# Two-layer graph attention on one core: two key tiles' weights of the second head group added by GpSimd, one sum visit fewer on TensorE, and a new order of the mixed phase

## The reference

```
# layer 0                                      # layer 1, per head
scores = (x Wq + bq)(x Wk + bk)^T / 16         logits = q k^T / sqrt(32) + log(clip(adj, 1e-8))
attn   = softmax(scores where adj != 0)        attn   = softmax(logits)
x1     = layernorm(x + (attn x) Wc)            out    = layernorm(x1 + (attn v) Wo + bo)
```

## Time and profile before

| | |
|---|---|
| median of three runs | 1208.09 us (1205.72 to 1211.17) |
| the profiled execution | 1208.68 us, span 1206.9 us |
| mean granted TensorE clock | 0.974 of full |
| busy share PE / DVE / POOL / ACT | 95% / 75% / 64% / 44% |
| PEld busy | 57% |
| period of one phase of the loop | 70.34 us |

### The profile page before, as it was taken

One profiled execution on the slowest core, in us unless ns is written; L12 is line 12 of the kernel. 1 busy time (PEld: TensorE's weight loads), 2 busy tenths in 40 slices (PEclk: granted clock), 3 DMA queues, 4 the chain that ended last, 5 costly groups with the idle time before them and its releaser, 6 DMA issues.

```text
span 1206.9 us, 21229 instructions
## 1 busy us (share of the span) xinstructions
PE 1142.7 (95%) x6458; PEld 684.8 (57%) x6474; DVE 905.3 (75%) x1718; ACT 526.8 (44%) x1021; POOL 766.5 (64%) x368
## 2 busy tenths in 40 slices
PE   7789999999999999999999999999999999999883
PEld 6555565655656565565646556564655656465431
DVE  4465886959688695968869596886959688795874
ACT  3234444545344454534445453444545344454431
POOL 1017487594948759494875949487594948759362
PEclk9889999999999999999999999999999999999786
DMA  3051331405133140513314051331405133140300
GB/s 131 1 138 37 106 88 43 133 18 141 50 107 85 42 133 18 142 50 107 84 43 132 18 142 50 109 83 44 131 18 144 48 109 83 44 131 18 96 27 18
DMA packets 69652, 94.67 MB, mean 78 GB/s; under 512 B 14081, under 2 KB 32769, under 8 KB 69634
## 3 DMA queue, kind: packets, MB, share of 16 engines
q1 hardware_dynamic: 69634, 94.44, 27.9%
HBM read 35.40 MB, written 8.39 MB: 36 GB/s over the span
## 4 chain that ended last, share of the span: by engine, by line
PE 41%; POOL 22%; DVE 20%; issue 12%; ACT 2%; DVEq 1%; POOLq 0%; DMA 0%; SPq 0%; ACTq 0%
POOL PR L1168 14%; DVE mx L1026 12%; PE misc L609 11%; PE scores L730 6%; PE misc L619 4%; PE values L753 3%; POOL z L1182 3%; PE misc L661 3%; PE misc L709 3%; POOL res L1151 3%; PE values L775 2%; PE denominators L753 2%; PE denominators L775 2%; DVE z L1108 2%; DVE st L1098 2%
## 5 line engine op out<-in xcount | busy, mean ns | idle before, releaser
L1168 POOL TENSOR_TENSOR PR<-PR,CLIP 128x1024 f32<-128x1024 f32 x232 | 572.6, 2494 | 339.7 <-ACT PR L868 315.7
L1026 DVE TENSOR_REDUCE mx<-misc 128x1 f32<-128x512 f32 x512 | 321.6, 680 | 92.5 <-PE misc L709 92.4
L868 ACT ACTIVATE PR<-scores 128x512 f32<-128x512 f32 x512 | 279.8, 603 | 225.3 <-PE scores L730 224.8
L730 PE MATMUL scores<-QS,KS 97*128 97x512 f32 x512 | 199.0, 463 | 7.5 <-issue 3.5
L753 PE MATMUL denominators<-PR,ones 128*32 128x512 f32 x1024 | 135.6, 601 | 6.3 <-POOL PR L1168 5.7
L730 PEld LDWEIGHTS scores<-QS,KS 97*128 97x128 f32 x512 | 89.0, 194 | 85.2 <-ACT PR L868 44.6
L753 PE MATMUL values<-PR,V 128*32 128x512 f32 x1024 | 133.2, 603 | 0.1
L709 PE MATMUL misc<-K1H,Q1H 32*128 32x512 f32 x512 | 120.9, 501 | 8.6 <-issue 3.0
L687 PE MATMUL misc<-U,P 128*128 128x257 f32 x512 | 121.8, 386 | 0.0
L1073 DVE RECIPROCAL sums_w<-sums_w 128x128 f32<-128x128 f32 x128 | 113.8, 923 | 4.2 <-ACT sums_w L881 4.2
L709 PEld LDWEIGHTS misc<-K1H,Q1H 32*128 32x128 f32 x512 | 49.2, 184 | 109.8 <-DVE mx L1026 52.7
(11 more groups left out here) (160 smaller groups left out, 1902.5 us busy)
## 6 DMA issues: line engine op xcount, KB each, us to landing
ADJ<-adj_t SPq DMA_DIRECT2D x16, 1024.0 KB, 6.1
QS<-Q1H SPq DMA_DIRECT2D x256, 64.0 KB, 2.0
KS<-K1H SPq DMA_DIRECT2D x256, 64.0 KB, 2.0
P<-x_t SPq DMA_DIRECT2D x16, 512.0 KB, 4.0
X<-x SPq DMA_DIRECT2D x16, 512.0 KB, 3.7
QS<-Q1L SPq DMA_DIRECT2D x128, 64.0 KB, 2.0
KS<-K1L SPq DMA_DIRECT2D x128, 64.0 KB, 2.0
out<-z SPq DMA_DIRECT2D x16, 512.0 KB, 2.9
```

Of the source, the lines that this page charges most:

```text
L730: pe.matmul(ST[n][:], KS[:, h, P * k:P * (k + 1)], QS[:, h, :], start=True, stop=True).then_inc(scores_filled, 1)
L868: act.activation(PR[quad % WEIGHT_BUFFERS][:, h, :], ST[n][:], ACT.Exp, scale=SCALE1).then_inc(exp_done, 1)
L1026: dve.tensor_reduce(mx1[:, g, h, t:t + 1], misc_bank(ph, "max1", g, n)[:], AX.X, ALU.max, negate=True).then_inc(misc_drained["dve"], 1)
L1168: pool.tensor_tensor(w, w, clipped, ALU.mult).then_inc(masked_pool, 1)
```

## The change

Four things change.

1. A new stage ("add", 5, pair): POOL adds the masked weights of quad 5 onto those of quad 4, in quad 4's buffer, in two instructions of 128x1024. It waits until `values1` of quad 4 has read that buffer and both quads are masked.
2. `denominators1` of quad 5 is gone; the one of quad 4, now later in the table, waits for the adds and sums both quads in one visit. PE makes 7 visits for denominators per graph in place of 8.
3. In `SCHEDULE` a second stage ("mask", 5, 1) moves one mask instruction per phase from POOL to DVE.
4. The whole `SCHEDULE` is reordered; in `LAST` only the stages around the adds change.

The rest of the code follows: waits for the masks are now made at every visit, and counts of denominators skip quad 5.

```
+ADDED = (5,)
 SCHEDULE = [
-    ("split", 0), ("split", 1), ("bias",), ("max1", 1, 0), ("q0", 0), ("reciprocal", 1, 0), ("q0", 1),
...
+    ("max1", 1, 0), ("split", 0), ("split", 1), ("max1", 1, 1), ("max1", 1, 2), ("bias",), ("q0", 0),
+    ("u", 0), ("reciprocal", 1, 0), ("q0", 1), ("scores1", 0, 0), ("u", 1), ("scores1", 0, 1),
...
 LAST = [
...
-    ("reciprocal", 0, 0), ("values1", 4), ("reciprocal", 0, 1), ("denominators1", 4), ("scores1", 6, 1),
-    ("values1", 5), ("scores1", 7, 0), ("mask", 6, 0), ("denominators1", 5), ("reciprocal", 0, 2),
-    ("scores1", 7, 1), ("values1", 6), ("reciprocal", 0, 3), ("mask", 7, 0), ("denominators1", 6),
-    ("high_output", 0), ("denominators1", 7), ("mask", 7, 1), ("values1", 7), ("normalise", 0),
-    ("sums_v", 1), ("sums_w", 1), ("low_output", 0),
+    ("add", 5, 0), ("reciprocal", 0, 0), ("values1", 4), ("reciprocal", 0, 1), ("scores1", 6, 1),
+    ("add", 5, 1), ("values1", 5), ("scores1", 7, 0), ("mask", 6, 0), ("reciprocal", 0, 2),
+    ("scores1", 7, 1), ("values1", 6), ("reciprocal", 0, 3), ("mask", 7, 0), ("denominators1", 4),
+    ("denominators1", 6), ("high_output", 0), ("denominators1", 7), ("mask", 7, 1), ("values1", 7),
+    ("normalise", 0), ("sums_v", 1), ("sums_w", 1), ("low_output", 0),
 ]
...
+            def wait_masked(ph, quad):
+                if masks(ph, False, quad) > (masks(ph, False, quad - 1) if quad else 0):
+                    pe.wait_ge(masked_pool, masks_before(ph, False) + masks(ph, False, quad))
+                if any(q == quad for q, _ in dve_masks(ph.kind)):
+                    pe.wait_ge(masked_dve, masks_before(ph, True) + masks(ph, True, quad))
...
             def values1(ph, quad):
-                sums1(ph, quad, PV, values_first(ph, quad)).then_inc(values_summed, 1)
+                wait_masked(ph, quad)
+                sums1(ph, quad, PV).then_inc(values_summed, 1)
 
             def denominators1(ph, quad):
-                sums1(ph, quad, DEN, not values_first(ph, quad)).then_inc(denominators_summed, 1)
+                if quad + 1 in ADDED:
+                    pe.wait_ge(weights_added, (ph.i * len(ADDED) + ADDED.index(quad + 1) + 1) * 2)
+                else:
+                    wait_masked(ph, quad)
+                sums1(ph, quad, DEN).then_inc(denominators_summed, 1)
...
+            def add(ph, quad, pair):
+
+                if pair == 0:
+                    pool.wait_ge(values_summed, ph.i * QUADS + quad)
+                    pool.wait_ge(masked_pool, masks_before(ph, False) + masks(ph, False, quad))
+                    if any(q in (quad - 1, quad) for q, _ in dve_masks(ph.kind)):
+                        pool.wait_ge(masked_dve, masks_before(ph, True) + masks(ph, True, quad))
+                w, total = (PR[q % WEIGHT_BUFFERS][:, 2 * pair:2 * pair + 2, :] for q in (quad, quad - 1))
+                pool.tensor_tensor(total, total, w, ALU.add).then_inc(weights_added, 1)
```

More of the change, by code:

```diff
@@ L73 @@
 SCHEDULE = [
-    ("split", 0), ("split", 1), ("bias",), ("max1", 1, 0), ("q0", 0), ("reciprocal", 1, 0), ("q0", 1),
[11 rows of a table removed]
-    ("scores1", 5, 0), ("denominators1", 3), ("sums_w", 0), ("mask", 5, 0), ("reciprocal", 0, 0),
-    ("scores1", 5, 1), ("values1", 2), ("denominators1", 4), ("values1", 3), ("sums_v", 0),
-    ("scores1", 6, 0), ("transpose", 0), ("transpose", 1), ("scores1", 6, 1), ("reciprocal", 0, 1),
[7 rows of a table removed]
+    ("max1", 1, 0), ("split", 0), ("split", 1), ("max1", 1, 1), ("max1", 1, 2), ("bias",), ("q0", 0),
+    ("u", 0), ("reciprocal", 1, 0), ("q0", 1), ("scores1", 0, 0), ("u", 1), ("scores1", 0, 1),
+    ("reciprocal", 1, 1), ("u", 2), ("reciprocal", 1, 2), ("max0", 0), ("reciprocal", 1, 3),
+    ("scores1", 1, 0), ("u", 3), ("normalise", 1), ("scores1", 1, 1), ("max0", 1), ("max0", 2),
+    ("scores1", 2, 0), ("max1", 1, 3), ("low_output", 1), ("max1", 1, 4), ("max1", 1, 5),
+    ("high_output", 1), ("max0", 3), ("skip_back",), ("scores1", 2, 1), ("project",), ("floor",),
[8 rows of a table added]
+    ("transpose", 0), ("transpose", 1), ("scores1", 6, 1), ("values1", 4), ("reciprocal", 0, 0),
+    ("reciprocal", 0, 1), ("reciprocal", 0, 2), ("mask", 5, 1), ("reciprocal", 0, 3), ("skip_front",),
[7 rows of a table added]
 ]
@@ L143 @@
 }
-BACK = ("residual", "mask", "scores1", "values1", "denominators1", "sums_v", "sums_w",
+BACK = ("residual", "mask", "add", "scores1", "values1", "denominators1", "sums_v", "sums_w",
         "reciprocal", "normalise", "high_output", "low_output", "skip_back")
@@ L421, in graph_of, with summed @@
             return ph.t if g == GROUPS - 1 else ph.i
+        def summed(quad):
+            return sum(1 for q in range(quad + 1) if q not in ADDED)
         def mask_operands(quad, pair):
@@ L731, in scores1, with sums1 @@
                               start=True, stop=True).then_inc(scores_filled, 1)
-            def sums1(ph, quad, bank, first):
+            def wait_masked(ph, quad):
[3 more added lines that the diff above has]
+                    pe.wait_ge(masked_dve, masks_before(ph, True) + masks(ph, True, quad))
+            def sums1(ph, quad, bank):
                 g, k = divmod(quad, T)
@@ L738, in sums1 @@
                     pe.wait_ge(z_added, ph.t * 2 + (1 if bank is PV else 2))
-                if first:
-                    if masks(ph, False, quad) > (masks(ph, False, quad - 1) if quad else 0):
-                        pe.wait_ge(masked_pool, masks_before(ph, False) + masks(ph, False, quad))
-                    if any(q == quad for q, _ in dve_masks(ph.kind)):
-                        pe.wait_ge(masked_dve, masks_before(ph, True) + masks(ph, True, quad))
-                    if quad == 0:
-                        pe.wait_ge(misc_drained["act"], misc.count_before(ph, "v", 1))
+                if quad == 0 and bank is PV:
+                    pe.wait_ge(misc_drained["act"], misc.count_before(ph, "v", 1))
                 if quad > 0 and k == 0:
@@ L1184, in output @@
                 pool.tensor_tensor(z[:], z[:], all_rows(S_B1), ALU.add).then_inc(out_ready, 1)
-            do = {"prepare": prepare, "residual": residual, "scores1": mask, "stats0": rstd0_of,
+            do = {"prepare": prepare, "residual": residual, "scores1": mask, "add": add, "stats0": rstd0_of,
                   "stats1": rstd1_of, "output": output}
```

8 lines of the change are left out of this document (3 added, 5 removed), and 33 rows, old and new, of the table SCHEDULE.

## The result

The changed kernel takes 1257.15 us (median of 4 runs, 1255.49 to 1261.48), the kernel before 1209.34 us beside it: ratio 1.041, 95% interval 1.0378 to 1.0441. It is slower by 4.1%, 48 us. I had forecast 1221, with 1194 to 1232 as the range: right in sign, wrong in size, outside the range.

The account below looks back on a forecast made before the run. It took a phase as one ring through POOL, PE, ACT and DVE, not PE alone, as the bound. From 1208.7 us, +0.7 per phase over 15 phases (+10) and +3 for the last back gave 1221, range 1194 to 1232.

Parts of the forecast that it names:

- From the first mask to xn: POOL's six masks through to xn: nothing added, two small covers of 0.31 and 0.20 us go, leaving xn 0.4 us later.
- the next term: The stretch from xn to the phase's end, where DVE's new mask was expected to wait for POOL's mask; +0.25 us.
- Start of the phase: From the first matmul to POOL's first mask: late XTL (0.55 us) and late exponentials (0.4) delay that mask 0.93 to 0.95.
- the second term: The stretch from POOL's first mask to xn, said to have nothing added or taken.
- the ring: A phase as one closed chain: POOL from first mask to xn, PE, ACT, DVE to last maximum, PE, ACT, next mask.
- z to xn: Part of the stretch up to xn: POOL's 0.20 us idle for quad 4's exponential goes, since POOL itself is late.
- From xn to the end: From xn to the phase's last maximum: later XNL, held DVE mask, adds and CLIP's wait; +0.25 us, range -0.4 to +2.0.
- the removed visit: One denominators visit fewer per graph on PE: booked as 0, with -1.04 us per phase as the low end.
- Rival 1: PE is the bound, so each graph gives back 0.86 to 1.04 us: 1191 to 1194 us; chance 0.24.
- The last back: The last graph's back: its denominators wait for POOL's second add, taken as +3 us.
- Rival 3: POOL or DVE bounds the whole ring: 1227 us by DVE's extra work, 1244 by POOL's adds; chance 0.15.
- The signs that I had named: Profile checks: period 71.0 us, first mask at 6.8, XNH behind exponentials, CLIP idle, PE busy down about 1 per phase.

Follow-up runs that it names:

- e1: Changed kernel, but in phases with a back the second head group's OTL is written as zero by a one-SBUF-input instruction; 1217.19 us, ratio 1.0067.
- e4: Changed kernel with the high output part on ACT and the low part on DVE one or two entries earlier; 1221.29 us, ratio 1.0126.
- k3: g2 with both splits ahead of the first maximum and u ahead of the first scores; 1249.02 us, ratio 1.0334.
- k4: k3 with one entry moved, the first of layer 0's maxima to behind head group 1's normalisation; 1213.80 us, ratio 1.003.
- g2: e4 with the last back (LAST) in the order of the kernel before, without adds there; 1215.07 us, ratio 1.0051.
- k5: k4 without the adds and without DVE's new mask, all eight denominators summed; 1218.93 us, ratio 1.0082.
- h1: e3 without DVE's new mask, so POOL makes all its masks and the two adds; 1232.86 us, ratio 1.02.
- k1: g2 with both splits of x ahead of the first maximum; 1213.01 us, ratio 1.0041.
- k2: g2 with the first context rows (u) ahead of the first scores; 1213.38 us, ratio 1.0035.
- f1: Kernel before with the first head group's low output part moved later on DVE, behind three maxima; 1239.69 us, ratio 1.0256.
- j1: g2 with the start of the phase as in the kernel before, up to quad 1's scores; 1245.19 us, ratio 1.0306.
- e2: Changed kernel's order alone: eight denominators, no adds, no new DVE mask, last back as before; 1264.07 us, ratio 1.0463.
- g1: e4 with splits and ABSENT ahead of the first maximum and u behind the second query projection; 1260.66 us, ratio 1.0425.
- g3: e4 with the edits of g1 and g2 together; 1254.17 us, ratio 1.0386.
- h2: Kernel before with only quad 5's second mask moved from POOL to DVE, behind the third reciprocal; 1308.99 us, ratio 1.0829.
- e3: Kernel before's order with the adds, DVE's new mask, CLIP three maxima later and the new last back; 1241.46 us, ratio 1.0277.
- h3: e3 with head group 0's normalisation six maxima later on DVE; 1251.66 us, ratio 1.0354.

## Why the prediction was right and wrong

- **The failed step is "From the first mask to xn".** It said "nothing is added or taken" and booked -0.31 for norm1 and -0.20 for POOL's idle time. Measured from POOL's first mask to z: 686.62 - 666.82 = 19.80 us, before 663.79 - 645.64 = 18.15, so +1.65 instead of -0.31. Nothing was added, but OTL was moved against POOL's masks: it asks 3.47 instead of 2.25 us behind the normalisation, just behind a mask's start. I had weighed such a meeting for one mask of the next term, with rows 8 in hand, and did not look at who meets whom in the stretch where POOL runs six masks without a gap. e1 and e4 take this away and give 1217 and 1221 us; k3 and k4 show it at another instruction. By the Trainium skill (SBUF — State Buffer, Who interferes with whom) a VectorE instruction with two SBUF inputs and a GpSimd instruction that reads SBUF exclude one another for a whole instruction; the trace agrees, 2.78 us instead of 0.68. I had used that rule where it cost 0.85 us and left it out where it cost 2.
- **The clock was in no term.** Seven of 13 phases are 1.53 us longer, those in which TensorE's clock falls after the wait: 10.7 us. With the 2.29 us of all 13 (29.8) and the first period (-1.0) that is the loop's 39.5.
- **Start of the phase, +0.93: right as a delay, too large as a cost.** It was 0.94, by the two delays that the term names. But undoing either half is worth 0.28 of period, and both together, in k4, 0.35: POOL then waits for the tail's statistics (0.45 us in k4, 0.17 in g2), as the second term should have asked. So the ring isn't as closed as I had it.
- **z to xn, -0.20: right** (20.20 against 20.46).
- **From xn to the end, +0.25, and the removed visit, 0.** The stretch took 25.81 us, before 25.82. XNH came behind the exponentials, XNL started 0.52 us later behind xn (710.74 - 706.82 against 687.65 - 684.25), and the add cost 2.37, as written. But DVE's new mask took 1.32 and was not held, CLIP did not wait, and the visit was not worth nothing: k5 against k4 gives 0.67 us per phase for the exchange as a whole. Rival 1's mechanism (PE's time counts) is real for about two thirds of a visit. What eats it is the order: k5, the new order with its meetings mended and no adds, is 0.88 us per phase slower than before. Of these, 0.72 lie between xn and PE's first projection of the next phase (26.97 us against 26.25), the stretch in which PE waits 0.82 for XNL. I had set XNL's delay against DVE's slack and not asked when PE wants it.
- **The last back, +3: mis-sized,** 6.2 by g2 against e4. I had POOL's masks and adds at 2.39; two of them took 3.3 beside DVE's masks, and three visits ran at the lower clock.
- **Rival 3** (POOL or DVE as the bound of the whole ring) gave the nearest number, 1244, for the wrong reason: with DVE 75% and POOL 64% busy, and all of the added work in place, e1 takes 1217 us. In the old order it is partly right, as h1 shows.
- That my number would have held with the lock that the kernel before has (e4: 70.88, +0.55 per phase, and 1221.3 us) is partly luck: -0.67 for the exchange and +1.2 for the order stood behind a sum of +0.7.
- **The signs that I had named** could not show the failure. POOL's first mask (6.86 us against 6.8), XNH, XNL, PE's waits and the wait in the last back came as written; CLIP's wait did not, PE's busy time rose by 9 us instead of falling, and the period was 72.6 or 74.2 instead of 71.0. None of the three that would have told me I was wrong occurred: none asked about DVE between the first mask and rstd. The prediction also has DVE full in two stretches; its rows show one.

Still open: whether PE's wait for XNL is what k5's 0.88 us are (every run of the new order has it, and none removes it), and what decides in which phases the clock falls.

## What to carry to other kernels

Where two engines shut one another out for whole instructions, a moved instruction is priced by where it arrives in the other's instruction, and that changes for every instruction behind an edit: lay both timelines side by side over the whole stretch in which the other engine runs without a gap, and ask for each two-input instruction whether it comes just behind a start. A price that jumps within 0.2 us of arrival makes the forecast two-sided: state both outcomes rather than one in the middle. Two small improvements can cost 34 us together (k1 and k2 against k3), so mend the arrival, not the load.

## What I had not expected of the hardware

- What a meeting costs DVE jumps within 0.2 us of arrival. The same 128x512 instruction, asked 0.23 us ahead of the next mask's start, still goes between the two masks (0.83 us, k2; 0.62 ahead, 1.21, k4), and then POOL's mask is the one that grows, by about 0.45 us. Asked within 0.02 us of the start, on either side, it waits for the whole mask (2.94, k3), and at 0.14 behind too (2.78). Where between 0.23 and 0.02 the switch lies no run shows.
- TensorE's clock in the 13 phases of the loop behind the first period, beside PE's longest regular wait. No fall: the kernel before (0.4 us), e1, e4, g2, k1, k2, k4, k5 (0.82), h1 (0.86). Falls: k3 (1.15 us) in 6 phases, f1 (1.5) 4, j1 (1.5) 8, the changed kernel (1.8) 7, e2 (1.8) 10, g1 (2.2) 5, g3 (2.2) 7, h2 (4.3) all 13. But also e3 (0.86) in 2, the last two, and h3, where no regular wait is over 0.65 us, in 6. So it isn't the length of the longest wait alone. In the changed kernel a fall costs 1.5 us of its phase, in g3 as little as 0.7.
